# All four layers: the clear behind each indirect transfer is taken out, and a transfer is issued when the last but one has landed

## What is computed

```python
edge_index = stack([src, dst])
h = maximum(layernorm(x), 0)
# layer 0: every edge fetches the row of its source node
Fj = h[src]                                   # 200,000 rows of 32 floats
msg = blocks of einsum(R(edge_weight), Y(edge_attr_3), Fj, C)
x = x + zeros.at[dst].add(msg)
h = maximum(layernorm(x), 0)
# layers 1 to 3: the same edges, widths 32 -> 128 -> 128 -> 32
def conv(h, W, b):
    hw = h @ W
    return segment_sum(hw[src] * norm[:, None], dst) + b
h = relu(conv(h, W1, b1)); h = relu(conv(h, W2, b2)); h = relu(conv(h, W3, b3))
return x + h
```

## Time and profile before

| | us |
|---|---|
| median of three runs | 5770.3 |
| lowest and highest run | 5766.4, 5771.2 |
| span of the profiled execution | 5779.7 |

### The profile page before, as it was taken

How to read it: one execution, slowest core, us unless ns; L and a number is a source line. 1 busy time by engine, 2 the same in 40 slices (tenths; PEclk the granted TensorE clock), 3 DMA queues, 4 the chain that set the end, 5 groups by cost and what they waited for, 6 DMA issues and landing times.

```text
span 5779.7 us, 179150 instructions
## 1 busy us (share of the span) xinstructions
PE 4258.6 (74%) x62463; PEld 3147.7 (54%) x62464; DVE 3608.0 (62%) x8469; ACT 2702.7 (47%) x6550; POOL 4889.1 (85%) x7276
## 2 busy tenths in 40 slices
PE   5777777777777777755555555889898889766666
PEld 3444444444444444444444444778787778554554
DVE  8777777777777777776666666333333334555555
ACT  4444444444444444466666666344444444433333
POOL 7888888888888888768888888688888889588886
PEclk9999999999999999955555555899989999767767
DMA  3111111111111111333332332332333333444444
GB/s 87 33 33 33 33 33 31 33 33 33 33 33 32 32 33 33 36 71 77 77 77 77 77 77 71 114 90 85 91 91 85 91 91 100 119 119 126 122 127 107
DMA packets 494970, 400.88 MB, mean 69 GB/s; under 512 B 269575, under 2 KB 454828, under 8 KB 493537
## 3 DMA queue, kind: packets, MB, share of 16 engines
q10 hardware_dynamic: 146996, 207.67, 10.6%
q0 software_dynamic: 115712, 109.02, 10.3%
q1 hardware_dynamic: 231536, 74.48, 5.9%
HBM read 375.52 MB, written 15.29 MB: 68 GB/s over the span
## 4 chain that ended last, share of the span: by engine, by line
POOL 50%; issue 40%; PE 5%; POOLq 2%; DVE 2%; DMA 1%; ACT 0%; DVEq 0%; SPq 0%
POOL rows L782 29%; POOL pause L762 21%; POOLq L761 2%; PE radial L2067 2%; PE psX L2082 1%; PE psT L2082 1%; PE sums L2153 1%; PE radial L2209 0%; DMA table<-arena 0%; PE radial L2222 0%; DMA rows<-table,idx 0%; DMA xn<-in_x 0%; POOLq L760 0%; PE radial L2008 0%; DVE rows L1827 0%
## 5 line engine op out<-in xcount | busy, mean ns | idle before, releaser
L782 POOL DMA_INDIRECT rows<-table,idx x3616 | 3636.6, 1006 | 803.0 <-POOL pause L762 483.7
L762 POOL MEMSET pause<- 128x256 f32 x3616 | 1234.8, 341 | 2.5
L1942 PEld LDWEIGHTS sums<-scratch,onehot 128*64 128x64 f32 x9408 | 789.7, 144 | 465.0 <-DVE scratch L1377 228.6
L2067 PE MATMUL radial<-arena,shared 128*32 128x96 bf16 (+1 forms) x31200 | 926.4, 266 | 154.2 <-DVE shared L1613 75.1
L1942 PE MATMUL sums<-scratch,onehot 128*64 128x264 f32 (+1 forms) x9408 | 984.1, 356 | 32.6 <-DVE scratch L1377 26.2
L2067 PEld LDWEIGHTS radial<-arena,shared 128*32 128x32 bf16 (+1 forms) x31200 | 664.8, 116 | 294.4 <-issue 72.0
L2153 PE MATMUL sums<-onehot,rows 128*128 128x80 f32 (+1 forms) x2844 | 371.0, 298 | 576.7 <-DMA rows<-table,idx 571.8
L1007 ACT CAST scratch<-radial 128x480 bf16<-128x480 f32 x860 | 476.9, 555 | 665.7 <-PE radial L2067 657.6
L1360 DVE TENSOR_TENSOR scratch<-radial,shared 128x768 f32<-128x768 f32 x784 | 743.4, 948 | 0.0
L1927 PE MATMUL radial<-shared 64*128 64x384 f32 x3136 | 730.5, 546 | 0.0
L880 ACT COPY shared<-rows 128x192 f32<-128x192 f32 x196 | 89.4, 456 | 1264.1 <-DMA rows<-table,idx 1262.9
(11 more groups left out here) (237 smaller groups left out, 5969.3 us busy)
## 6 DMA issues: line engine op xcount, KB each, us to landing
scratch<-places_d ACTq DMA_DIRECT2D x242, 800.0 KB
rows<-table,idx POOLq DMA_INDIRECT x3616
shared<-in_edge_weight SPq DMA_DIRECT2D x390, 128.0 KB, 2.9
idx<-in_src SPq DMA_DIRECT2D x451, 4.0 KB
table<-arena SPq DMA_DIRECT2D x24, 256.0 KB, 2.8
table<-arena SPq DMA_DIRECT2D x2, 1176.0 KB, 10.6
accT<-in_edge_attr SPq DMA_DIRECT2D x2, 1152.0 KB
table<-arena SPq DMA_DIRECT2D x24, 96.0 KB, 2.0
```

The costliest lines, as they stand in the source:

```text
L762: nc.gpsimd.memset(pause[:, :], 0.0).then_inc(made, 1)
L782: (pool.indirect_dma_start(rows_3[:, r, j, :] if n in (1, 3) else rows[:, r, j, 0:WIDTH[n]], None, tables[n], bass.IndirectOffsetOnAxis(ap ...
L1942: last = nc.tensor.matmul(there, onehot[:, u % 2, 4 * h + t, 0:SW], taken_from, start=(h + q + part == 0), stop=(h == 1 and q == 1 and par ...
L2067: last = nc.tensor.matmul(d, from_src[n][:, h, i, t, :], table_of(n, s), start=True, stop=True, tile_position=(0, 32 * i))
```

## The change

Five things change together, for all layers:

- the tile `pause`, its clear and the wait for the last clear are gone;
- in front of each transfer `j` of a group POOL waits until the last but one transfer has landed, `wait_ge(gathered[j % 2], count)`. In the first and the last turn of a layer the count is a constant, in the loops it is in one of two registers, raised by 16 after each wait;
- the four landing semaphores become two: transfers with even `j` add to one, those with odd `j` to the other;
- SP, ACT and TensorE, which waited for one landing semaphore, now wait for both (`wait_for_rows`), to half the count each: the same group as before must have landed;
- the first two transfers of the program wait for no landing.

```diff
-        gathered = [sem(f"gathered{u}") for u in range(UNROLL)]
+        gathered = sems("gathered", 2)

-        def rows_gathered(step, n, u, plus):
-
-            return step.times(step.groups // UNROLL * 16 * TPG, 16 * TPG * (rounds_before(n) + u // UNROLL + plus))
+        def wait_for_rows(eng, step, n, u):
+
+            count = step.times(step.groups * 16 * TPG // 2, 16 * TPG // 2 * (sum(GATHERED[:n]) + u + 1))
+            for half in range(2):
+                eng.wait_ge(gathered[half], count)

-            pauses = pool.alloc_register("pauses")
-
-            def pause_between(step, n, u, j):
+            landed = [pool.alloc_register(f"landed{half}") for half in range(2)]
+
+            def last_but_one_landed(step, n, u, j):

                 if step.peeled:
-                    before = TPG * (sum(GATHERED[:n]) + step.it * step.groups + u) + j
+                    before = TPG // 2 * (sum(GATHERED[:n]) + step.it * step.groups + u) + j // 2
                     if before:
-                        pool.wait_ge(made, 9 + before)
+                        pool.wait_ge(gathered[j % 2], 16 * before)
                 else:
-                    pool.wait_ge(made, pool.snap(pauses))
-                    pool.reg_add(pauses, pauses, 1)
-                nc.gpsimd.memset(pause[:, :], 0.0).then_inc(made, 1)
+                    pool.wait_ge(gathered[j % 2], pool.snap(landed[j % 2]))
+                    pool.reg_add(landed[j % 2], landed[j % 2], 16)

                         for j in range(TPG):
                             col = j % 2 * KS + j // 2
+                            last_but_one_landed(step, n, u, j)
                             (pool.indirect_dma_start(rows_3[:, r, j, :] if n in (1, 3) else rows[:, r, j, 0:WIDTH[n]], None, tables[n],
                                                      bass.IndirectOffsetOnAxis(ap=idx[:, r, col:col + 1], axis=0))
-                                 .then_inc(gathered[r], 16))
-                            pause_between(step, n, u, j)
+                                 .then_inc(gathered[j % 2], 16))
```

More of the change, by code:

```diff
@@ L61 @@
 PAD_REL = -1000.0
-PAUSE = 256
 assert NG % UNROLL == 0 and PTAIL * KS == ETAIL and PTAIL <= P and NG == 2 * NB
@@ L295, in gnn_kernel @@
         one = sb("one", [P, 1])
-        pause = sb("pause", [P, PAUSE])
         flag = sb("flag", [P, 1])
@@ L615, in load_idx @@
                 if n > 0 or not (first and u < UNROLL):
-                    sp.wait_ge(gathered[r], rows_gathered(step, n, u, 0))
+                    wait_for_rows(sp, step, n, u - UNROLL)
                 if n == 0 and (step.it * UNROLL + u == NG - 1 if step.peeled else False):
@@ L806, in gathers @@
                     pool.reg_mov(turn[u], 2 * (LOOP[n][0] // UNROLL - 1) if n else 0)
-                pool.reg_mov(pauses, 9 + TPG * (sum(GATHERED[:n]) + LOOP[n][0]))
+                for half in range(2):
+                    pool.reg_mov(landed[half], 16 * TPG // 2 * (sum(GATHERED[:n]) + LOOP[n][0]))
                 sweep(pool, body, n)
@@ L874, in layer0 @@
                                          ACT.Relu, bias=b1c[:, :], scale=w1c[:, :]).then_inc(hid_ready[u % 2], 1)
-                    act.wait_ge(gathered[u], rows_gathered(step, 0, u, 1))
+                    wait_for_rows(act, step, 0, u)
                     if not (first and u < 2):
@@ L2144, in gathered_sum @@
                         far_rows[j] = (rows if n == 2 else rows_3)[0:counts[j], r, j, 0:w] if counts[j] else None
-                    pe.wait_ge(gathered[r], rows_gathered(step, n, u, 1))
+                    wait_for_rows(pe, step, n, u)
                     far_windows(n, far)
```

## The result

The changed kernel takes 6763.3 us against 5769.2 before: 1.172 times as long, 95% interval 1.171 to 1.174. The forecast was 5640 us, so it missed by 1,123 us, and with the wrong sign. The profiled execution has a span of 6760.3 us.

What follows compares the result with a forecast made beforehand. The prediction took POOL's own step to bound the kernel almost everywhere. Layers 0 to 3 gave -204 + 0 + 8 + 65 = -131 us, from 5770.3 to about 5640 us, range 5480 to 5800.

Steps and rivals of the forecast that it cites:

- What bounds the kernel: All layers: POOL's own step, 1.483 to 1.576 us, sets the pace; in layer 2 TensorE at 1.40 is close.
- Landings: Time from a transfer's issue to its landing: means of 2.56, 2.75, 2.95 and 2.98 us in layers 0 to 3.
- The wake-up: Time from a landing to the start of POOL's waiting transfer: taken as 0.16 us, bounds 0.10 and 0.25.
- forecast's own formula: POOL's step is half of landing plus wake-up, unless issue alone is longer, with 0.04 us added for late landings.
- entered at nothing: Remaining effects counted as zero: POOL's sequencer work unchanged, second waits of SP, ACT and TensorE hidden, SP's loads unchanged.
- The price of a late landing: POOL's transfers: a late landing also holds the other semaphore's transfers standing behind it; 0.04 us a step added.
- A: Layers 1 to 3: landings that meet place-list loads cost their full delay, so slower, about 5865 us; chance 0.21.
- turning point: Where landing plus wake-up exceeds two of today's steps: landings of 2.85, 2.99 and 2.81 us in layers 1 to 3.
- B: All layers: landings up to 0.33 us quicker without the clear, so much faster, about 5080 us; chance 0.06.
- C: All layers: landings equal two of today's steps less the wake-up, so no change that counts, 5770 us; chance 0.08.
- D: Layer 0: the pace passes to TensorE or DVE, steps of 1.45 instead of 1.40 us, 5715 us; chance 0.10.
- The rule of the Trainium skill: GpSimd-issued DMA: 2.0 us plus bytes over 436e3, 2.04 us in layer 0; the forecast went by the row's 2.33.

Runs made afterwards that it cites:

- e2: The kernel before without its clear, the clear's wait and registers, and with no wait for landings in their place: 4917.4 us, 0.853 of before.
- e3: The changed kernel with POOL's turns written out, so all counts are constants and the landing wait can ride on the transfer: 6198.2 us, 1.075 times before.
- e4: The changed kernel with a twenty-fifth of each place list loaded in the loops of layers 1 to 3: 6559.9 us.
- e8: e3 with a twenty-fifth of each place list in the loops of layers 1 to 3 and edge weights loaded 16 wide in layer 0's loop: 5960.4 us.

## Why the prediction was wrong

**What bounds the kernel**: right. POOL's step set the pace, and e2 shows it from the other side: 0.24 us less a step in the mean of all layers took 852 us off. One part was wrong: the forecast has TensorE at 1.40 us a step in layer 2, with POOL hardly ahead. In e2 TensorE is busy 882 of 900 us there, the step is 1.313, and the granted clock is 0.99, where it was 0.91 before (the last view of this document).

**Landings**: right in size. The forecast means were 2.56, 2.75, 2.95 and 2.98 us, and those of the changed kernel are 2.51, 2.87, 2.89 and 3.06. For layers 1 to 3 three rows stood behind them, so that is partly luck.

**The wake-up**: this is the step that failed first. The 0.16 us was no wake-up of the transfer in the earlier trace rows. That transfer is the eighth of its group, and line 776, in front of it in time, is the next group's wait for its buffer: in the program it stands behind the transfer, on which the sequencer's work was already done. So the row shows the 0.16 us between a clear and the next transfer once more, and the bound of 0.25 us, from the same pieces, was too short for the same reason. The trace of before does hold rows of a transfer that is taken up only after a wait, at the start of each layer, where POOL waits for the landing of the table; the forecast says that there is no wait for a landing in front of an indirect transfer. Layer 1 (chain: start us, us, what):

```profile
2489.22 13.08 DMA table<-arena
...
2502.57 0.03 POOLq L807
2502.60 0.71 issue
2503.31 0.95 POOL rows L782
```

From the sequencer's last instruction to the transfer it is 0.71 us here, and 0.82, 0.70 and 0.71 in layers 0, 2 and 3. In the loops of the changed kernel the wake-up measures 0.76 us, on 3,040 of 3,616 transfers (47 turns of 32, six of 96, six of 96, six of 64), and 0.26 on most others. By the forecast's own formula that is 0.30 x 3,040 + 0.05 x 576 = 941 us of the 1,123 missed. The sentence that failed stands under "entered at nothing": the sequencer's work stays what it was. The instructions did stay the same, but what they can run beside did not.

**The price of a late landing**: this failed second. I added 0.04 us a step. e3, where the wake-up is 0.26, stands at 1.503, 1.718, 1.746 and 1.844, and half of forecast landing plus 0.26 would be 1.41, 1.51, 1.61 and 1.62; 0.09 to 0.22 a step are left. The landings in the trace of e3 divide this. Their mean is 2.54, 2.91, 2.96 and 3.14 us, so the forecast was 0.16 too low in layers 1 and 3, which is 0.08 a step; the longer wake-up of the first of a group is 0.03. The rest is the order: a transfer also stands behind the one before it, whatever its own semaphore says. I take each start as the later of two times: the start before it plus the bare issue (1.25 us, or the issue plus 0.30 where that was longer), and the measured landing of the last but one plus the wake-up (0.26 us, 0.74 for the first of a group). The steps then come to 1.480, 1.706, 1.732 and 1.824, within 0.03 of what was measured, while half of mean landing plus wake-up gives 1.43, 1.62, 1.64 and 1.73. So the order costs 0.05 to 0.10 us a step and not 0.04. That the bare issue is 1.25 us and not 1.11 (without a clear 0.30 us and not 0.16 stand between two transfers, e2) is only 0.01 to 0.03 of it. With 0.76 us for every wake-up the same working gives the steps of the changed kernel, within 0.03. That late landings weigh is measured: 203 us by e4, and the chain of e3 in layer 3 runs through them, from 2.43 to 4.91 us:

```profile
5502.06 4.91 DMA rows<-table,idx
5506.98 0.26 issue
...
5510.52 2.43 DMA rows<-table,idx
...
5516.93 4.33 DMA rows<-table,idx
```

**Rivals.** A had the right place, and that a held transfer holds both chains, with 5865 us; as far as landings alone go, e3 is its measure, 6198. How much of that the place lists make is open: layers 1 to 3 of e3 stand 478 us above before, and the small loads of e8 give 189 of it back. I gave it 0.21, and called landings "that close" to its turning point; what I didn't see is that the same turning point, two of today's steps less the wake-up, lies at 2.31, 2.26, 2.40 and 2.22 us in the four layers for a wake-up of 0.75, below the median landing of each (2.38, 2.47, 2.56 and 2.48 in the changed kernel). B is refuted by e2's landings, C and D by the steps. None of the four had the wake-up as its mechanism.

**The rule of the Trainium skill** ("DMA: Bandwidth & Descriptors", "Anatomy of one DMA — SWDGE (gpsimd) path", an estimate of 2.04 us) is below even the quick landings that the views of the runs show, 2.33 to 2.43 us from the start of issue; deciding by the row was right. What mattered was in neither.

## What to carry to other kernels

POOL's wait cost more than the 0.26 us of a bare wake-up where it stood in front of an instruction that POOL's sequencer needs time for: what used to be prepared beside other work was done after it. Put such a wait on the instruction itself where its count can be a constant, or wait for an event so old that it is over. Take the price of a wake-up from a place in the trace where the engine had really stood still, as at a layer's start here. Before replacing a throttle by a cleverer one, run the kernel without any: here the throttle was 15% of the time.

## What was not expected of the hardware

- POOL's sequencer takes about 0.7 us from a wait in front of an indirect transfer to the transfer's start (0.48 + 0.03 + 0.19, or 0.70), and 0.26 when the transfer carries the wait.
- Indirect transfers issued back to back start every 1.25 us (0.94 issue, 0.30 between), and with no limit but four groups of buffers no issue got slower. Landings stayed as they were in layer 0 and became longer in layers 1 and 3, by 0.4 us for a group's eighth transfer.
- Between two transfers without a clear 0.30 us pass; between a clear and a transfer it was 0.16, so the clear's net price was 0.19 us in an undisturbed step and not 0.49.
- With e2's faster steps TensorE is granted its full clock (2.4 GHz) in the stretches of layers 0 and 2, 1.00 and 0.99, where it had 0.92 and 0.91 before; it is busy 1652 of 1880 us and 882 of 900 (the first columns are the stretch and PE's busy time; the last clock, DMA share, GB/s):

```profile
100.00:1980.00 1880.00, 1652.44 (x13732) 1066.80 (x13732) 1747.31 (x3387) 1031.13 (x3003) 1423.48 (x1498) 1.00 0.20 41
...
3150.00:4050.00 900.00, 881.81 (x15781) 781.17 (x15770) 379.49 (x718) 462.35 (x1389) 689.43 (x692) 0.99 0.37 106
```
